# Rotary queries and keys of a local attention, projected with head dimensions on partitions and joined by SBUF-to-SBUF DMAs

## The reference

```
xn = layernorm(x)
s  = xn + sum over 8 heads of relu(causal(Q K^T)) / 512 @ V          # stage A
f  = routed attention(xn) + local attention(xn), averaged by counts   # stages C and B
out = x + s * silu(f)
```

```
q, k, v = split(ln(xn) @ w_qkv.T)                 # heads of 64
q = q * cos + rotate_half(q) * sin                # the same for k
sim = q_window @ [k_previous, k_window].T * 64**-0.5, masked
local = softmax(sim) @ [v_previous, v_window] @ w_lo.T
rotate_half(t): t1, t2 = halves of 32;  concatenate([-t2, t1])
```

## Time and profile before

| | |
|---|---|
| time, median of 3 runs (lowest to highest) | 861.8 us (857.28 to 861.93) |
| time of the profiled execution | 858.44 us |
| its span, first to last instruction | 856.6 us |
| mean granted TensorE clock | 0.991 |
| busy share PE, DVE, ACT, POOL | 95%, 60%, 51%, 27% |
| instructions | 18723 |

### The profile page before, as it was taken

The page is one execution under the profiler, slowest core; times in us unless marked ns, Lnnn a source line. Parts: engine busy times, 40 slices in busy tenths (PEclk is TensorE's granted clock), DMA queues, the critical chain, the costliest instruction groups (busy, mean ns, idle before and its releaser), DMA issues.

```text
span 856.6 us, 18723 instructions
## 1 busy us (share of the span) xinstructions
PE 815.2 (95%) x6709; PEld 665.2 (78%) x6709; DVE 512.4 (60%) x1136; ACT 435.4 (51%) x1573; POOL 228.5 (27%) x369
## 2 busy tenths in 40 slices
PE   3899999999998999999999999999999999999994
PEld 3588888878886777777778778787878788787874
DVE  6321333356626888788788785656464564646577
ACT  3242444432233656656666666656464665647461
POOL 2200000000002874434434434433132313323211
PEclk9899999999999999999999999999999999999997
DMA  8500000000000000000000000000000000000001
GB/s 246 231 1 1 1 0 0 0 0 0 1 1 2 2 2 2 3 2 2 2 2 2 2 2 2 1 2 0 0 0 0 1 1 2 1 0 0 0 9 42
DMA packets 10256, 12.11 MB, mean 14 GB/s; under 512 B 2128, under 2 KB 8784, under 8 KB 9552
## 3 DMA queue, kind: packets, MB, share of 16 engines
q1 hardware_dynamic: 10192, 11.24, 3.8%
HBM read 10.19 MB, written 1.05 MB: 13 GB/s over the span
## 4 chain that ended last, share of the span: by engine, by line
PE 88%; DVE 4%; ACT 3%; SPq 2%; issue 1%; POOL 1%; DVEq 1%; DMA 0%; POOLq 0%; ACTq 0%
PE ps L675 8%; PE ps L687 8%; PE ps L722 7%; PE ps L926 6%; PE ps L982 5%; PE ps L965 5%; PE ps L949 5%; PE ps L844 4%; PE ps L910 4%; PE ps L830 4%; PE ps L821 4%; PE ps L787 4%; PE ps L662 3%; PE ps L855 3%; PE ps L799 3%; PE ps L656 3%
## 5 line engine op out<-in xcount | busy, mean ns | idle before, releaser
L504 POOL TENSOR_TENSOR stage<-stage 128x1024 f32<-128x1024 f32 x32 | 75.5, 2358 | 124.7 <-DVE stage L1581 118.9
L1265 ACT ACTIVATE early<-ps,nmC 128x128 f32<-128x128 f32 (+1 forms) x224 | 77.8, 368 | 53.7 <-DVE dnC L1637 53.2
L1210 ACT ACTIVATE stage<-ps,nmB 128x128 f32<-128x128 f32 x256 | 89.7, 384 | 3.9 <-DVE nmB L1569 3.9
L675 PE MATMUL ps<-stage,early 128*128 128x128 f32 (+2 forms) x448 | 87.3, 323 | 0.0
L687 PE MATMUL ps<-stage 128*128 128x128 f32 (+2 forms) x448 | 85.9, 321 | 1.4 <-DVE stage L1456 1.4
L675 PEld LDWEIGHTS ps<-stage,early 128*128 128x128 f32 x448 | 65.2, 191 | 25.1 <-issue 15.0
L687 PEld LDWEIGHTS ps<-stage 128*128 128x128 f32 x448 | 65.1, 192 | 11.8 <-issue 1.6
L1451 DVE COPY stage<-ps 128x512 f32<-128x512 f32 x32 | 22.1, 691 | 85.2 <-PE ps L662 85.2
L556 POOL TENSOR_SCALAR stage<-iota,kvcol 128x128 f32<-128x128 f32 (+1 forms) x112 | 66.9, 607 | 10.6 <-issue 10.6
L1632 DVE TENSOR_REDUCE nmC<-ps 128x4 f32<-128x512 f32 (+1 forms) x56 | 36.6, 653 | 48.1 <-PE ps L949 47.6
L965 PE MATMUL ps<-early,stage 128*128 128x512 f32 (+1 forms) x112 | 59.4, 612 | 3.7 <-ACT early L1277 3.7
(11 more groups left out here) (201 smaller groups left out, 1780.4 us busy)
## 6 DMA issues: line engine op xcount, KB each, us to landing
x<-in_x SPq DMA_DIRECT2D x4, 256.0 KB, 3.8
stage<-in_cq SPq DMA_DIRECT2D x1, 1024.0 KB, 5.8
stage<-in_ck SPq DMA_DIRECT2D x1, 1024.0 KB, 7.7
stage<-in_cv SPq DMA_DIRECT2D x1, 1024.0 KB, 9.8
stage<-in_co SPq DMA_DIRECT2D x1, 1024.0 KB, 11.7
early<-in_wqk SPq DMA_DIRECT2D x1, 1024.0 KB, 15.1
out<-stage SPq DMA_DIRECT2D x4, 256.0 KB, 2.3
stage<-in_Wq SPq DMA_DIRECT2D x1, 512.0 KB, 6.1
```

The source lines that it names most:

```text
L504: pool.tensor_tensor(rot[:, u % 2].rearrange("p a b -> p (a b)"), r1[:, u % 2].rearrange("p a b c -> p (a b c)"), r2[:, u % 2].rearrange(" ...
L675: t = pe.matmul(ps[:, 4 + s, at:at + q1 - q0], xnT[:, b, m * P:(m + 1) * P], yT[:, b % 2, q0:q1], start=True, stop=True)
L1210: t = act.activation(pB[:, u % 2, at, :], ps[:, 4 + h, i * P:(i + 1) * P], ACT.Exp, bias=nmB[:, u % 2, at:at + 1], accum_out=rsB[:, u % 2, ...
L1265: act.activation(pC[:, k, hg, 0:n], ps[:, 5 + k, hg * P:hg * P + n], ACT.Exp, bias=nmC[:, k, hg:hg + 1], accum_out=rsC[:, k, hg:hg + 1])
```

## The change

- The unit of the first steps is now s, one for the queries (even s) or the keys (odd s) of **four** heads, that is of the pairs of units 2j and 2j+1 with j = s // 2. `b_project(s)` makes two products of 512 token columns: the first 32 dimensions (half f = 0) of the four heads on the 128 partitions of bank 0, the other 32 (f = 1) in bank 1. The weights are put in that order once by POOL, which also multiplies those of the queries by 64**-0.5.
- `b_rope(s)` multiplies both banks by one cosine and one sine table (1024 elements each). POOL's `add(s)` makes the rotated halves, a difference and a sum of 512 elements; for keys the windows are reordered there.
- SP issues 8 SBUF-to-SBUF DMAs a step, 32 partitions x 512 elements (64 KB) each, which place the halves so that the 64 dimensions of a head stand on neighbouring partitions (`qkT`). `b_turn`, `b_turned` and `b_kturned` are gone. `b_scores(u)` waits for the placed steps 2j and 2j+1.
- The loop works three steps ahead: project, rope and add of s = u+3. `b_out` comes a unit later, and the DVE copy of the turned probabilities goes to ACT.
- The first two units of stage A's last head keep their products of weights; the four of the last two units are done between stage A and stage B. Step 1 is projected inside the end of stage A.
- The tail computes silu(f) as f/2 * (1 + tanh(f/2)): the counts are doubled, ACT takes Tanh, and DVE has one fused operation in place of sum, reciprocal and product. ACT loads the table set `exp_and_others` before stage B.

```diff
-            sp.dma_start(wqk, dram["wqk"]).then_inc(s_wqk, 16)
+            sp.dma_start(wqk_in.rearrange("p a k h f d -> p a (k h f d)"), dram["wqk"]).then_inc(s_wqk, 16)
+            for s in range(NU):
+                j, qk = divmod(s, 2)
+                if j >= 2:
+                    for h in range(2):
+                        sp.wait_ge(sim_out[h], 4 * (j - 1))
+                for f in range(2):
+                    sp.wait_ge(rot_in, 2 * s + f + 1)
+                    for a in range(2):
+                        for h in range(2):
+                            at, to = W * a + DH // 2 * h, DH * h + DH // 2 * f
+                            sp.dma_start(qkT[to:to + DH // 2, j % 2, qk, a, :],
+                                         rot[at:at + DH // 2, s % 2, f, :]).then_inc(qk_placed[qk], 16)
...
+            pool.wait_ge(s_wqk, 16)
+            for qk in range(2):
+                for f in range(2):
+                    to = wqk[:, qk, f].rearrange("p j (a h d) -> p (j a) h d", a=2, h=2)
+                    t = pool.tensor_scalar(to, wqk_in[:, :, qk, :, f, :], (SCALE, 1.0)[qk], None, ALU.mult)
+            t.then_inc(s_wq, 1)
...
-            def add(u):
-                pool.wait_ge(roped, u + 1)
-                if u >= 2:
-                    pool.wait_ge(qkT_out, u - 1)
-                    pool.wait_ge(norm_in, 2 * (u - 1))
-                pool.tensor_tensor(rot[:, u % 2].rearrange("p a b -> p (a b)"),
-                                   r1[:, u % 2].rearrange("p a b c -> p (a b c)"),
-                                   r2[:, u % 2].rearrange("p a b c -> p (a b c)"), ALU.add).then_inc(rot_in, 1)
+            def add(s):
+                k, qk = s % 2, s % 2
+                pool.wait_ge(sT_in, 2 if s == 0 else B)
+                pool.wait_ge(roped, s + 1)
+                if s >= 2:
+                    pool.wait_ge(qk_placed[qk], PLACED * (s // 2))
+                for f in range(2):
+                    to, a, b = rot[:, k, f, :], rc[:, k, f, :], rs[:, k, 1 - f, :]
+                    if qk == 1:
+                        to = to.rearrange("p (r i t) -> p i r t", r=2, t=W)
+                        a, b = (v.rearrange("p (i r t) -> p i r t", r=2, t=W) for v in (a, b))
+                    pool.tensor_tensor(to, a, b, (ALU.subtract, ALU.add)[f]).then_inc(rot_in, 1)
...
+            add(0)
+            pool.drain()
             pool.wait_ge(pv_done, B)
             pool.memset(vS[W:P, :, 0, :], 0.0).then_inc(vS_zero, 1)
             pool.drain()
-            add(0)
             add(1)
             shifted(0)
+            add(2)
             for u in range(NU):
-                if u + 2 < NU:
-                    add(u + 2)
+                if u + 1 < NU:
+                    shifted(u + 1)
+                if u + 3 < NU:
+                    add(u + 3)
                 if u < B:
                     pick_columns(u)
-                if u + 1 < NU:
-                    shifted(u + 1)
...
-            def b_project(u):
-                b, p = divmod(u, PAIRS)
-                if u > 0:
-                    pe.wait_ge(roped, u)
-                to = ps[:, 0:2].rearrange("p k (a n) -> p (k a) n", a=2)
-                for k in range(BLK):
-                    t = pe.matmul(to[:, k, :], xlnT[:, b, k * P:(k + 1) * P], wqk[:, p, :],
-                                  start=True, stop=True)
+            def b_project(s):
+                j, qk = divmod(s, 2)
+                b, p = divmod(2 * j, PAIRS)
+                if s > 0:
+                    pe.wait_ge(roped, s)
+                for f in range(2):
+                    t = pe.matmul(bank(f), wqk[:, qk, f, p // 2, :], xlnT[:, b, :], start=True, stop=True)
...
+            b_project(1)
...
-            def b_turn(u):
-                pe.wait_ge(rot_in, u + 1)
-                if u >= 2:
-                    pe.wait_ge(pT_in, u - 1)
-                    pe.wait_ge(pT_in_v, u - 1)
-                for i in range(2):
-                    for t4 in range(BLK):
-                        t = pe.transpose(ps[:, 2 + i, t4 * P:(t4 + 1) * P], rot[:, u % 2, t4, i * P:(i + 1) * P],
-                                         ident[:])
-                t.then_inc(qkT_out, 1)
...
-                pe.wait_ge(qT_in, u + 1)
-                pe.wait_ge(kT_in, u + 1)
-                flat = kT.rearrange("p r i t -> p (r i t)")
+                j, a = divmod(u, 2)
+                for qk in range(2):
+                    pe.wait_ge(qk_placed[qk], PLACED * (j + 1))
+                qT, flat = qkT[:, j % 2, 0, a, :], qkT[:, j % 2, 1, a, :]
+                kT = flat.rearrange("p (r i t) -> p r i t", r=2, t=W)
...
+            def late_weights(n):
+                for job in range(W_W2C + LATE // 2 + n, W_W2C + LATE // 2 + n + 2):
+                    weights(job, prior=UNITS * HA)
             b_values(0)
-            pe.wait_ge(sT_in, B)
-            b_turn(0)
+            late_weights(0)
+            code_columns()
+            b_project(2)
+            late_weights(2)
             pe.wait_ge(qcode_in, 1)
             pe.wait_ge(w_in, W_W2C + 8)
             pe.wait_ge(vS_zero, 1)
                 b_scores(u)
                 if u > 0:
                     b_turn_probs(u - 1)
-                if u + 2 < NU:
-                    b_project(u + 2)
-                else:
+                if u > 1:
+                    b_out(u - 2)
+                if u > 0:
+                    b_mix(u - 1)
+                if u + 1 < NU:
+                    b_values(u + 1)
+                if u + 3 < NU:
+                    b_project(u + 3)
+                elif u + 2 >= NU:
...
-            def b_turned(u):
-                act.wait_ge(qkT_out, u + 1)
-                act.activation(qT, ps[:, 2, :], ACT.Copy).then_inc(qT_in, 1)
...
             def b_probs(u):
-                act.wait_ge(pT_out, 2 * u + 1)
-                act.activation(pTB[:, 0:BLK], ps[:, 2].rearrange("p (i n) -> p i n", n=P), ACT.Copy).then_inc(pT_in, 1)
+                for h in range(2):
+                    act.wait_ge(pT_out, 2 * u + h + 1)
+                    act.activation(pTB[:, BLK * h:BLK * (h + 1)], ps[:, 2 + h].rearrange("p (i n) -> p i n", n=P),
+                                   ACT.Copy).then_inc(pT_in, 1)
 
             def b_mixed(u):
                 act.wait_ge(ax_out, 2 * (u + 1))
-                act.activation(axB, ps[:, 6, :], ACT.Copy).then_inc(ax_in, 1)
+                if u >= 2:
+                    act.wait_ge(out_done, u - 1)
+                act.activation(axB[:, u % 2, :], ps[:, 6, :], ACT.Copy).then_inc(ax_in, 1)
...
+            act.preload_act_table_set("exp_and_others")
             b_valued(0)
-            b_turned(0)
+            for job in range(W_W2C + LATE // 2, W_W2C + LATE):
+                weights(job)
...
-                act.activation(eN[:, b % 2], yN[:, b % 2], ACT.Exp, scale=-1.0).then_inc(e_ready, 1)
+                act.activation(eN[:, b % 2], yN[:, b % 2], ACT.Tanh).then_inc(e_ready, 1)
...
-            def b_rope(u):
-                k = u % 2
-                dve.wait_ge(qk_out, u + 1)
-                if u >= 2:
-                    dve.wait_ge(rot_in, u - 1)
-                src = ps[:, 0:2].rearrange("p k (a h e) -> p (k a) h e", a=4, e=DH)
...
-                dve.tensor_tensor(r1[:, k], src, cos[:].rearrange("p k c e -> p (k c) e").unsqueeze(2).broadcast_to(
-                    [P, 2 * BLK, 2, DH]), ALU.mult)
-                dve.tensor_tensor(r2[:, k, :, :, 0:e2], src[:, :, :, e2:DH], table(sin, 0), ALU.mult)
-                dve.tensor_tensor(r2[:, k, :, :, e2:DH], src[:, :, :, 0:e2], table(sin, e2), ALU.mult).then_inc(roped, 1)
-            def b_kturned(u):
-                dve.wait_ge(qkT_out, u + 1)
-                dve.tensor_copy(kT, ps[:, 3, :].rearrange("p (i r t) -> p r i t", r=2, t=W)).then_inc(kT_in, 1)
+            def b_rope(s):
+                k = s % 2
+                dve.wait_ge(qk_out, s + 1)
+                if s >= 2:
+                    dve.wait_ge(rot_in, 2 * (s - 1))
+                for to, table in ((rc, cos), (rs, sin)):
+                    t = dve.tensor_tensor(to[:, k], ps[:, 0:2], table[:].unsqueeze(1).broadcast_to([P, 2, N]), ALU.mult)
+                t.then_inc(roped, 1)
 
             dve.wait_ge(w_in, W_NULL + 1)
             b_rope(0)
+            b_rope(1)
...
-            def b_probs(u):
-                dve.wait_ge(pT_out, 2 * u + 2)
-                dve.tensor_copy(pTB[:, BLK:], ps[:, 3].rearrange("p (i n) -> p i n", n=P)).then_inc(pT_in_v, 1)
...
-            b_rope(1)
+            b_rope(2)
             for u in range(NU):
                 b_max(u)
-                if u > 0:
-                    b_probs(u - 1)
-                if u + 2 < NU:
-                    b_rope(u + 2)
-                else:
+                b_norm(u, 0)
+                b_norm(u, 1)
+                if u + 3 < NU:
+                    b_rope(u + 3)
+                elif u + 2 >= NU:
                     at = 2 * (u + 2 - NU)
```

(12 more changed lines are left out.)

126 lines of the change are left out of this document (53 added, 73 removed).

## The result

| | before | after |
|---|---|---|
| time, median (lowest to highest) | 859.6 us (857.28 to 861.93) | 901.5 us (895.89 to 910.3) |
| profiled execution, its span | 858.44, 856.6 us | 906.86, 904.9 us |
| mean granted TensorE clock | 0.991 | 0.957 |

The ratio is 1.047, with a 95% interval of 1.039 to 1.055: 42 us slower by the medians, 40 by the ratio. Forecast were 12 us less, with 836 to 865 as the range. An execution that took over 1.5% more than the fastest of its kernel, with a lower granted clock, is left out of every ratio (here the one of 910.3 us), while medians hold all executions.

The account below looks back on a forecast made before the run. PE's work bounds the kernel now; after the change the DMA chain sets 15.4 us a pair against PE's 14.3. Stage B -8.4 and tail -4.0 make -12.4 us: 848 us forecast, range 836 to 865.

Parts of the forecast that it names:

- scores of unit 2: Stage B's start: scores of unit 2 were to begin at 289.9 us, 3 us later than before.
- 14 pairs, length at full clock: Stage B's loop: each pair of units was to last 15.4 us, with PE waiting 1.1 us at each even unit.
- The step between issues: SP's queue: seven steps from the first to the eighth placement issue, taken at 0.45 us each, 0.475 by loads in a row.
- The landing: Placement DMAs: issue to landing estimated at 1.6 us for 64 KB, with ends of 1.3 and 2.3.
- Rival 4: PE in stage B: waits of 1.1 us at even units lower the granted clock, time over 900; chance 0.03.
- rivals 1: DMA chain longer, landing 2.3 and step 0.475: pair 16.3, time about 861, no change; chance 0.30.
- The stage's start: Between stages A and B: weight products move there, PE waits for sT; scores of unit 0 at 275.5, unit 2 at 289.9.
- the chain itself: From an even unit's scores through projection, rope, sum, eight issues and landing to the next even unit's scores: 15.4 us.
- the floor of 7.15: PE's own work per unit in stage B once b_turn's 0.93 us leaves the 8.08.
- rope and sums: Stage B: DVE's rope at 2.37 us and POOL's two sums at 1.26 us each.
- the tail's 3.7: Kernel's end: fused gate without reciprocal saves 3.7 us after the last output product; 0.3 for an earlier wait makes 4.0.
- Rival 3: Placements queue on the DMA engines or the keys' strided sum doubles; pair 17.3 gives 875 us; chance 0.13.

Follow-up runs that it names:

- The lone DMAs: Kernel before with lone and successive DMAs on SP's queue during stage A into an unread buffer; issues out of SBUF took 0.51 to 0.61 us alone.
- the six placements: Kernel after with six placement DMAs a step instead of eight, first halves of both heads in one DMA; 873.0 us, ratio 1.008 to the kernel before.
- The filled waits: Kernel after with repeated mask products on PE where it would wait for placements or sT; 879.8 us, ratio 1.023 to the kernel before.
- Start the chain sooner: Kernel after with step u+3 projected right behind the turned probabilities, rope ahead of norms, add ahead of shifted; 868.8 us, ratio 1.014 to the kernel before.
- the three-slot kernel: Kernel after with a third slot for placed queries and keys and the loop four steps ahead; 833.7 us, ratio 0.970 to the kernel before.

## Why the prediction was wrong

The sum gave 846.0 for the profiled execution; it took 906.9. The 60.9 us between, by the prediction's own steps (the last line ends with DVE's last residual sum):

| step | predicted | measured | us |
|---|---|---|---|
| scores of unit 2 | 289.9 | 301.92 | 12.0 |
| 14 pairs, length at full clock | 15.4 | 17.27 | 26.2 |
| the same, later placements | 0 | 0.23 a pair | 3.2 |
| the same, clock | 0 | 1.04 a pair | 14.5 |
| unit 30 to stage C | 14.0 | 16.1 | 2.1 |
| stage C and the tail | 322.0 | 324.7 | 2.7 |

- **The step between issues failed.** "I take 0.45", from loads out of DRAM at 0.43. The first step is 0.55 and the six others 0.63, so the seven take 4.35 us and not 3.15: 1.20 us more a pair, 16.8 in the 14 pairs. Even the upper end, 0.475, was too low: both ends came from the same row. The lone DMAs and the six placements show the price, and that it is one for each instruction. This is a mis-sized term, in the right place.
- **The landing** was 2.02 for 1.6: 0.42 a pair, inside the bounds of 1.3 and 2.3. The Trainium skill ("DMA: Bandwidth & Descriptors", Anatomy of one DMA), from whose figures the prediction worked out 2.15 us, was nearer than my 1.6, and the trace agrees with it within 0.15 us for 64 KB. I had subtracted all slices with traffic of the 256 KB store from its 2.3; the lone DMAs of 128 and 256 KB land alike. The rest of the 1.87, 0.25, lies between the engines: SP's first issue starts 0.21 later behind the scores than I had it.
- **The clock failed with it, and took more.** Behind waits of the length that came it took 14.5 us in the pairs, 3.0 in unit 30 (10.21 us for 7.24) and 4.2 at the stage's start, 21.7 in all. Rival 4 had the waits lower it, at 0.03 and with a time over 900, which is what came, but with waits of 1.1 us, which did not. My reason against it was the earlier trace rows: a stretch with more idle time that holds 1.00. That idle time is a sum of short waits, of which the longest is this one, in the kernel before:

```profile
273.52 1.99 PE L722 MATMUL ps<-early 128*128 128x256 f32 x8 [1.48 <-DVE stage L1532]
```

  So the rows spoke for waits of the predicted size only, and there they may stand: with six placements, behind waits of 1.47, the clock held all eight times. But the waits were 2.7 us and more, and behind ten of the 15 the next unit was longer. The filled waits show it as cause. The mistake was to judge this rival at the forecast's wait alone, and not at that of rivals 1 and 3, where it would have added its price to theirs.
- **The stage's start.** Of the 12.0, 6.3 are stage A's clock and not the change's. "Start the chain sooner" begins stage B in the same order, with the clock of the kernel before in stage A, and puts the scores of unit 0 at 274.52, where I had said 275.5: the order of the start was right, and too dear by 1. Another 4.2 are the clock behind the wait of 2.61 us for `sT`: the first weight products take 2.07 us for 1.16, and from stage A's last product to the scores of unit 0 it takes 18.49 us instead of 14.26. In the two other kernels the clock held behind waits of 2.40 and 2.61. The last 2.5 are the longer way from unit 0 to unit 2 (16.92 us for 14.4), the same in the three-slot kernel.
- **Right were** the chain itself, with every engine on it in order and the wait only at even units; the floor of 7.15 (7.24 measured with the chain hidden); rope and sums; that the keys' strided sum costs nothing extra (1.28 for both); the tail's 3.7.
- **Stage C** cost 2.4 us more than before (577.53 to 898.6 at PE's last product, against 527.90 to 846.6). The traces show where: PE waits 1.57 us there for DVE's last copy of picked queries, which now stands behind the norms, and the output product that the prediction counted ahead of stage C (0.86) runs inside it. The prediction had put the first at nothing.

```profile
577.53 0.39 PE L924 MATMUL ps<-xhat,ident 128*128 128x128 f32 x2
579.48 1.78 PE L940 MATMUL ps<-early,G 128*128 128x224 f32 x8 [1.57 <-DVE early L1588]
```

- **Rival 3** gave 875 for a pair of 17.3, which is what came (17.27), and the kernel with filled waits took 879.8. Its reason was wrong: the transfers do not queue behind each other, the instructions that issue them do.

The error in method: the chain was 15.4 against a floor of 14.3, two of its prices, the step between issues and the landing, came from rows of other kinds of DMA, and each microsecond over the floor counted 15 times. At such a place the range has to be taken from the sum of the upper ends, and beyond them: that sum was 16.3, and what came was 17.3, and what the clock takes.

## What to carry to other kernels

Before a copy through an engine is replaced by DMAs, count the instructions on the issuing queue, not the bytes: here each SBUF-to-SBUF one put 0.63 us into the chain, and a step needs 4.35 + 2.0 us from its first issue to its last landing. Such a chain is harmless if it is given one more buffer and one more step ahead: the same instructions then went from 5% slower to 3% faster. And a wait of PE in each round can cost more than its length: behind ten of 15 waits of 2.7 us and more the products ran at half the clock for a while, 1.3 us and more a time.

## What the runs showed of the hardware that was not expected

- Issue on SP's queue: 0.59 us out of SBUF for 32 to 128 partitions, 0.35 (one) and 0.43 out of DRAM.
- Landing out of SBUF into SBUF, from the start of the issue: 1.7 us for 16 KB, 2.0 for 64, 2.3 for 128 and 256.
- The granted clock fell to 1.2 GHz in the unit behind ten of the changed kernel's 15 waits at even units (2.72 to 4.17 us), and behind none of eight of 1.47 us with six placements; of four waits of 2.72 or 2.73 us in a row, from 473 to 525 us, it fell behind none. At the stage's start it fell behind a wait of 2.61 us and in the three-slot kernel held behind one as long. What decides between like waits stays open.
- DVE's product of two SBUF operands takes 1.80 us instead of 0.69 beside POOL's sums.
- Single issues of up to 1.79 us among those of 0.59 (up to 1.97 in other kernels with eight placements a step); cause open.
